# Attention A's relative shift: one write and one read per tile in place of two alternating column halves

## Chip, cores and metric

The kernel runs on one core of one Trainium2 chip. The metric is the time of one execution in device microseconds, lower being better; the median of several runs is quoted.

## What is computed

A block of four layers on x of shape (4, 2048, 256): x plus attention A, plus a feed-forward layer, plus attention B, plus the same feed-forward layer, each on a layer norm of x. Attention A has 16 heads of dimension 16 and relative positions, and it is the layer that the change touches:

```python
def _relative_shift(x):
    b, h, s, _ = x.shape
    x = jnp.pad(x, ((0, 0), (0, 0), (0, 0), (1, 0)))
    x = x.reshape(b, h, s + 1, s)
    return x[:, :, 1:, :].reshape(b, h, s, s)
...
content_score = jnp.einsum('bhsp,bhtp->bhst', q + u, k)
pos_score = jnp.einsum('bhsp,htp->bhst', q + v, pos)
pos_score = _relative_shift(pos_score)
score = (content_score + pos_score) / jnp.sqrt(jnp.float32(P))
weights = jax.nn.softmax(score, axis=-1)
out = jnp.einsum('bhst,bhtp->bhsp', weights, val)
```

The shift puts a zero in front of every row of the 2048 x 2048 matrix of position scores and then reads the same numbers again in rows of 2048. It moves elements between rows by an amount that differs from row to row.

## The kernel before

The four batches run one after the other, and each goes through attention A, feed-forward, attention B and feed-forward. In attention A a batch has 16 heads, a head has 16 tiles of 128 query rows by 2048 keys in f32 (1 MB), so there are 256 tiles to a batch and 1024 in all.

The shift is done by a trip through device memory. The position scores of a tile are computed by TensorE (L522), copied from PSUM to the buffer `rel` in chunks of 512 columns, three by ScalarE (L639) and one by VectorE (L693), and written by DMA to `rel_rows` with a row pitch of S + 1 = 2049 elements. They are read back to the buffer `z` with a row pitch of 2048, starting one row on, which is the shift. `rel` and `z` hold four tiles each (`RING = 4`). VectorE then adds the content scores from PSUM to `z` in two halves of 1024 columns and takes the row maxima (L658, `score`), GpSimd subtracts the maximum (L716), TensorE transposes `z` (L541, `turn`), ScalarE takes the exponential into `pT` (L631) and TensorE multiplies by the values (L562).

Every engine runs the same list of steps s (`in_order`): a prologue of nine steps, a loop of 64 steps (four heads) taken three times, and 64 last steps. In step s each part works on another tile: the position scores on tile s + 9 (`R_LEAD`), the read of `rel_rows` on s + 6 (`Z_LEAD`), the content scores and `score` on s + 4 (`C_LEAD`), the transposes and exponentials on s + 2, the values on s + 1. So a tile is read back three steps after it is written, and scored two steps after it is read.

SyncE (SP) issues every DMA. Its `step` does, in this order: wait until the `z` slot is free (tile n - 4 is transposed, `t_full[3]`), and until tiles n and n + 1 are written (`rel_out`); read half 0 of tile n (L760); wait for the copy of chunk 1 and write half 0 of tile r (L769); read half 1 of tile n; wait for the copies of chunks 2 and 3 and write half 1 of tile r; then, in 12 of 16 steps, two loads of 64 KB for a coming head, and one of 256 KB in one more. A half is 128 rows of 1024 f32, so a transfer has 128 packets of 4 KB, and every one of the 16 DMA engines gets 8 of them. A finished transfer adds 16 to its semaphore, so a tile adds 32 to `rel_out[k]` and 32 to `rel_in[k]` (`moved`). `score` waits for both reads; the copies into a `rel` slot wait for both writes of the tile that had it four tiles ago.

Of the kernel before, what the change touches and what calls it, by code (L numbers as in the profile page):

```python
# [26 lines left out]
P = 128  # L27
# [4 lines left out]
S = 2048  # L32
NT = S // P
# [9 lines left out]
FLAT = S * (S + 1)  # L43
RING = 4
# [10 lines left out]
R_ACT = [0, 1, 2]  # L55
R_DVE = 3
R_FIRST = 3
HB = 4
NB = 2
G = HB * NT  # L60
# [6 lines left out]
OB = 4  # L67
# [12 lines left out]
def program(nc, a, out, nb=4, nh=H):  # L80

    ctx = ExitStack()
    with ctx:
        def sb(name, shape, dt=F32):
            return ctx.enter_context(nc.sbuf_tensor(name, shape, dt))
# [4 lines left out]
        def sem(name):  # L90
            return ctx.enter_context(nc.semaphore(name))
# [8 lines left out]
        rel_d = nc.dram_tensor("rel_rows", (NB, FLAT), F32).ap()  # L100
# [8 lines left out]
        rel = sb("rel", [P, RING, S])  # L109
        z = sb("z", [P, RING, S])  # L110
# [105 lines left out]
        rel_out = [sem(f"rel_out{k}") for k in range(RING)]  # L216
        rel_in = [sem(f"rel_in{k}") for k in range(RING)]
# [6 lines left out]
        QK_INC = 16 * 2 * len(QPART)  # L224
# [6 lines left out]
        def settle(e):  # L231

            e.sem_inc(waited, 1)
# [257 lines left out]
        def in_order(e, b, step):  # L491

            def counts(p):
                return Counts(*(e.snap(b * (nh // HB * per) + p * per)
                                for per in (G, G // OB, 32 * G // RING, HB // NB * QK_INC, HB // NB * 16)))

            with e.Fori(0, 1) as p:
                base = counts(p)
                for s in range(-R_LEAD, 0):
                    step(p, base, s, lambda n: n >= 0)  # L500
            with e.Fori(0, GROUPS - 1) as p:
                base = counts(p)
                for s in range(G):
                    step(p, base, s, lambda n: True)
            with e.Fori(GROUPS - 1, GROUPS) as p:
                base = counts(p)
                for s in range(G):
                    step(p, base, s, lambda n: n < G)

        def moved(base, n):  # L510

            return base.moves + 32 * (n // RING + 1)

        def pe_attn_a(e, b):

# [104 lines left out]
        def act_attn_a(e, b):  # L620

            def step(p, base, s, here):

                r, t = s + R_LEAD, s + T_LEAD
                if here(t):
                    if s >= 0:

                        e.wait_ge(AA["pv_done"], base.tiles + (t - 1))
                    for q in range(4):
                        e.wait_ge(t_full[q], base.tiles + (t + 1))  # L630
                        e.activation(pT[:, t % 2, q * CH:(q + 1) * CH], rg[:, T_BANK[q], :], ACT.Exp,  # L631
                                     scale=SCALE).then_inc(p_ready[q], 1)
                if here(r):
                    if s >= 0 or r >= RING:

                        e.wait_ge(rel_out[r % RING], moved(base, r - RING))
                    for c in R_ACT:
                        e.wait_ge(r_full[c], base.tiles + (r + 1))
                        e.activation(rel[:, r % RING, c * CH:(c + 1) * CH], rg[:, R_BANK[c], :],  # L639
                                     ACT.Copy).then_inc(r_copied[c], 1)  # L640

            in_order(e, b, step)

        def dve_attn_a(e, b):

            def score(p, base, n, half, first):

                ready, read = (("lo_ready", "lo_read"), ("hi_ready", "hi_read"))[half]
                mx = (mlo, mhi)[half][:, n % 2:n % 2 + 1]
                if half == 0:  # L650
                    e.wait_ge(rel_in[n % RING], moved(base, n))
                    if not first:

                        e.wait_ge(AA["nmax_ready"], base.tiles + (n - 1))
                e.wait_ge(AA[ready], base.tiles + (n + 1))
                settle(e)
                zs = z[:, n % RING, 2 * half * CH:2 * (half + 1) * CH]
                e.tensor_tensor_reduce(out=zs, in0=scf[:, 2 * half * CH:2 * (half + 1) * CH], in1=zs, scale=1.0,  # L658
                                       scalar=-3.0e38, op0=ALU.add, op1=ALU.max, accum_out=mx).then_inc(AA[read], 1)
# [65 lines left out]
        def load_pair(e, q, k, q_src, k_src, h, slots, done):  # L725

            for a in slots:
                load_part(e, q, q_src, h, a, QPART[a], done)
                load_part(e, k, k_src, h, a, KPART[a], done)

        def load_v(e, h, hd, done):
            e.dma_start(v_s[hd].rearrange("p t w -> p (t w)"),
                        v_d[bass.ds(h, 1)].rearrange("a p w -> (a p) w")).then_inc(done, 16)

        def sp_attn_a(e, b):

            every = range(SLOTS)
            load_pair(e, qv_s[0], pos_s[0], qv_d, pos_d, 0, every, qv_loaded[0])
            load_pair(e, qu_s[0], k_s[0], qu_d, k_d, 0, every, AA["qk_loaded0"])
            load_v(e, 0, 0, AA["v_loaded0"])  # L740
            load_pair(e, qv_s[1], pos_s[1], qv_d, pos_d, 1, every, qv_loaded[1])

            def read_ready(p, base, n, fresh, last):

                k = n % RING
                if not fresh:

                    e.wait_ge(t_full[3], e.snap(base.tiles + (n - RING + 1)))
                    settle(e)
                e.wait_ge(rel_out[k], e.snap(moved(base, n)))  # L750
                settle(e)
                if not last:
                    e.wait_ge(rel_out[(n + 1) % RING], e.snap(moved(base, n + 1)))
                    settle(e)

            def read_half(n, half):

                k, hd, i0, c0 = n % RING, n // NT % NB, n % NT * P, half * S // 2
                shifted = bass.AP(tensor=rel_d.tensor, offset=hd * FLAT + (i0 + 1) * S + c0, ap=[[S, P], [1, S // 2]])
                e.dma_start(z[:, k, c0:c0 + S // 2], shifted).then_inc(rel_in[k], 16)  # L760

            def write_half(base, n, half):

                k, hd, i0, c0 = n % RING, n // NT % NB, n % NT * P, half * S // 2
                for c in ((R_DVE, R_ACT[-1]) if half else (R_ACT[1],)):
                    e.wait_ge(r_copied[c], e.snap(base.tiles + (n + 1)))
                    settle(e)
                there = bass.AP(tensor=rel_d.tensor, offset=hd * FLAT + i0 * (S + 1) + 1 + c0, ap=[[S + 1, P], [1, S // 2]])
                e.dma_start(there, rel[:, k, c0:c0 + S // 2]).then_inc(rel_out[k], 16)  # L769

            def next_heads(p, base, s, final):

                hd, at = s // NT, s % NT
                nxt = (hd + 1) % NB
                if at in range(1, 7) and not (final and hd + 1 >= HB):
                    if at == 1:
                        e.wait_ge(AA["hi_ready"], e.snap(base.tiles + hd * NT + C_LEAD))
                        settle(e)
                    load_pair(e, qu_s[nxt], k_s[nxt], qu_d, k_d, e.snap(p * HB + (hd + 1)), (at - 1,),
                              AA[f"qk_loaded{nxt}"])  # L780
                if at == 7 and not (final and hd + 1 >= HB):
                    e.wait_ge(AA["pv_done"], e.snap(base.tiles + (hd * NT + V_LEAD)))
                    settle(e)
                    load_v(e, e.snap(p * HB + (hd + 1)), nxt, AA[f"v_loaded{nxt}"])
                if at in range(8, 14) and not (final and hd + 2 >= HB):
                    if at == 8:
                        e.wait_ge(r_full[2], e.snap(base.tiles + (hd + 1) * NT))
                        settle(e)
                    load_pair(e, qv_s[hd % NB], pos_s[hd % NB], qv_d, pos_d, e.snap(p * HB + (hd + 2)), (at - 8,),
                              qv_loaded[hd % NB])  # L790

            def step(p, base, s, here):

                n, r = s + Z_LEAD, s + R_LEAD
                final = not here(G)
                if here(n):
                    read_ready(p, base, n, s < 0 and n < RING, n % NT == NT - 1)
                for half in range(2):
                    if here(n):
                        read_half(n, half)  # L800
                    if here(r):
                        write_half(base, r, half)
                if s >= 0:
                    next_heads(p, base, s, final)

            in_order(e, b, step)


# [640 lines left out]
```

## Time and profile before

| | us |
|---|---|
| median of 3 runs | 11098.51 |
| lowest and highest of them | 11085.86, 11107.45 |
| the profiled execution's own time | 11115.23 |
| its span, first to last instruction | 11113.4 |
| of it: PE, DVE, ACT, POOL busy | 9422.7, 6258.0, 6687.5, 2944.3 |
| TensorE's mean granted clock | 0.947 |

The span is cut by the profile's second part into 40 slices of 278 us, with the busy tenths of each engine, TensorE's granted clock, the mean busy share of the 16 DMA engines and the GB/s that they moved. The groups by line, the waits, the timeline and the table of windows can each be asked of any stretch of the span. In a table of windows the column DMA share is the time of all packets over 16 engines' time; consecutive packets overlap a little, so that it can pass 1.

### The profile page before, as it was taken

Reading aid. Unit: us, or ns where it says so; the run is one execution under the profiler, and the core shown is the slowest. Engines: PE = TensorE matmul, PEld = TensorE weight load, DVE = VectorE, ACT = ScalarE, POOL = GpSimd, SP = SyncE. Lnnn points to the kernel's source line nnn. Section 1 sums busy time; section 2 is a strip of 40 time slices with the busy share of each in tenths; the row PEclk is TensorE's granted clock in tenths of the full one; section 3 lists DMA queues with packets and bytes.
Section 4 is the critical chain, followed back from the end, with each engine's and each line's share of the span. In section 5 each row is a group of like instructions: output and inputs, shape, how many; then the busy total and the mean of one; then the engine's idle time right before and its main releaser. Section 6 shows DMA issues by size and latency. Waiting matters only on the chain. (4 is left out here: it accounts for less than half of the span.)

```text
span 11113.4 us, 271423 instructions
## 1 busy us (share of the span) xinstructions
PE 9422.7 (85%) x95520; PEld 6711.5 (60%) x95520; DVE 6258.0 (56%) x14730; ACT 6687.5 (60%) x11009; POOL 2944.3 (26%) x3520
## 2 busy tenths in 40 slices
PE   5888888999688888899968888889996888888999
PEld 3665665666465666566646656656663565665666
DVE  3655663765365566376446556637644565663764
ACT  3666663765466666376546666637644666663764
POOL 2333332001233333200123333310012333331001
PEclk7999999999899999999989999999998999999999
DMA  6999992000699999100069999911007999991100
GB/s 240 378 363 366 381 378 87 26 25 16 233 377 366 361 379 380 59 25 25 16 254 380 367 362 382 365 46 27 23 18 265 373 372 362 379 357 48 27 22 26
DMA packets 747623, 2482.45 MB, mean 223 GB/s; under 512 B 111745, under 2 KB 133761, under 8 KB 745921
## 3 DMA queue, kind: packets, MB, share of 16 engines
q1 hardware_dynamic: 746176, 2463.84, 60.3%
q8 instruction: 826, 13.53, 0.5%
q14 instruction: 621, 5.08, 0.1%
HBM read 1280.34 MB, written 1183.07 MB: 222 GB/s over the span
## 5 line engine op out<-in xcount | busy, mean ns | idle before, releaser
L658 DVE CUSTOM_DVE_ANT_0 z<-sc,z 128x1024 f32<-128x1024 f32 x2048 | 2496.5, 1220 | 1848.5 <-DMA z<-rel_rows 1608.0
L716 POOL TENSOR_SCALAR z<-z,nmax 128x1024 f32<-128x1024 f32 x2048 | 2277.8, 1123 | 4028.5 <-DVE nmax L668 4028.5
L631 ACT ACTIVATE pT<-rg 128x512 f32<-128x512 f32 x4096 | 2445.9, 598 | 738.7 <-PE rg L541 679.5
L541 PE MATMUL rg<-ident,z 128*128 128x128 f32 x16384 | 2527.0, 277 | 77.0 <-issue 68.3
L639 ACT ACTIVATE rel<-rg 128x512 f32<-128x512 f32 x3072 | 1721.1, 596 | 1407.2 <-PE rg L522 1401.8
L541 PEld LDWEIGHTS rg<-ident,z 128*128 128x128 f32 x16384 | 1990.3, 142 | 784.6 <-ACT rel L639 294.4
L522 PE MATMUL rg<-pos_s,qv_s 96*128 96x512 bf16 x4096 | 1590.8, 396 | 1021.4 <-DVE rel L693 901.6
L1013 DVE CUSTOM_DVE_ANT_0 z<-sc,mask 128x1024 f32<-128x1024 f32 (+7 forms) x1536 | 1359.1, 910 | 227.0 <-PE sc L832 173.9
L952 ACT ACTIVATE pT<-rg 128x512 f32<-128x512 f32 (+3 forms) x1792 | 928.4, 550 | 763.0 <-PE rg L885 751.0
L522 PEld LDWEIGHTS rg<-pos_s,qv_s 96*128 96x128 bf16 x4096 | 478.7, 118 | 1498.0 <-DVE rel L693 1150.9
L960 ACT ACTIVATE z<-z,nmax 128x128 f32<-128x128 f32 (+15 forms) x1024 | 1226.6, 1198 | 89.0 <-POOL nmax L978 76.7
L885 PE MATMUL rg<-ident,z 128*128 128x128 f32 x8704 | 1256.8, 289 | 0.0
L562 PE MATMUL op<-pT,xnT 128*32 128x128 f32 x32768 | 1129.9, 279 | 0.0
L885 PEld LDWEIGHTS rg<-ident,z 128*128 128x128 f32 x8704 | 972.0, 145 | 254.9 <-issue 188.4
L562 PEld LDWEIGHTS op<-pT,xnT 128*32 128x32 f32 x32768 | 847.2, 111 | 243.9 <-issue 214.0
L866 PE MATMUL op<-pT,xnT 128*32 128x128 f32 x17408 | 791.9, 283 | 149.6 <-ACT pT L952 45.5
L693 DVE COPY rel<-rg 128x512 f32<-128x512 f32 x1024 | 702.4, 686 | 183.1 <-PE rg L522 142.4
L866 PEld LDWEIGHTS op<-pT,xnT 128*32 128x32 f32 x17408 | 503.2, 110 | 299.1 <-DVE attn L988 120.6
L534 PE MATMUL sc<-k_sb,xnT 96*128 96x512 bf16 x2048 | 631.2, 390 | 0.0
L534 PE MATMUL sc<-xnT 96*128 96x512 bf16 x2048 | 615.1, 381 | 0.7 <-DVE mlo L658 0.7
L1032 DVE COPY pT<-rg 128x512 f32<-128x512 f32 (+3 forms) x768 | 428.6, 558 | 297.3 <-PE rg L885 288.2
L700 DVE COPY po_sb<-op 128x128 f32<-128x128 f32 x1024 | 298.8, 292 | 494.1 <-PE op L562 493.2
(93 smaller groups left out, 8161.5 us busy)
## 6 DMA issues: line engine op xcount, KB each, us to landing
rel_rows<-rel SPq DMA_DIRECT2D x2048, 512.0 KB, 7.2
z<-rel_rows SPq DMA_DIRECT2D x2048, 512.0 KB, 7.1
xnT<-qu_parts SPq DMA_DIRECT2D x792, 64.0 KB, 2.3
xnT<-v_heads SPq DMA_DIRECT2D x132, 256.0 KB, 4.3
v_heads<-rel SPq DMA_DIRECT2D x8, 4096.0 KB, 12.5
k_sb<-k_parts SPq DMA_DIRECT2D x408, 64.0 KB, 2.3
qv_s<-qv_parts SPq DMA_DIRECT2D x384, 64.0 KB, 6.2
pos_s<-pos_parts SPq DMA_DIRECT2D x384, 64.0 KB, 7.2
```

Of the source, the lines that this page charges most:

```text
L522: e.matmul(rg[:, R_BANK[c], :], qv_s[hd][:, i0:i0 + P], pos_s[hd][:, c * CH:(c + 1) * CH], start=True, stop=True).then_inc(r_full[c], 1)
L534: mm = e.matmul(sc[:, c, :], qu_s[hd % NB][:, i0:i0 + P], k_s[hd % NB][:, c * CH:(c + 1) * CH], start=True, stop=True)
L541: mm = e.transpose(rg[:, T_BANK[q], (j - 4 * q) * P:(j - 4 * q + 1) * P], z[:, n % RING, j * P:(j + 1) * P], ident[:, :])
L562: mm = e.matmul(po[32 * g:32 * g + 32, :], v_s[hd % NB][:, j, :], pT[:, n % 2, j * P:(j + 1) * P], start=j < 4, stop=j + 4 >= NT)
L631: e.activation(pT[:, t % 2, q * CH:(q + 1) * CH], rg[:, T_BANK[q], :], ACT.Exp, scale=SCALE).then_inc(p_ready[q], 1)
L639: e.activation(rel[:, r % RING, c * CH:(c + 1) * CH], rg[:, R_BANK[c], :], ACT.Copy).then_inc(r_copied[c], 1)
L658: e.tensor_tensor_reduce(out=zs, in0=scf[:, 2 * half * CH:2 * (half + 1) * CH], in1=zs, scale=1.0, scalar=-3.0e38, op0=ALU.add, op1=ALU.ma ...
L716: e.tensor_scalar(zs, zs, 1.0, nmax[:, n % 2:n % 2 + 1], ALU.mult, ALU.add).then_inc(AA[done], 1)
L866: mm = e.matmul(po[32 * g:32 * g + 32, :], v_s[t // NT % NB][:, j, :], pT[:, t % 2, j * P:(j + 1) * P], start=j < 4, stop=j + 4 >= nj)
L885: mm = e.transpose(rg[:, B_BANK[q], (j - 4 * q) * P:(j - 4 * q + 1) * P], z[:, t % RING, j * P:(j + 1) * P], ident[:, :])
L960: e.activation(z[:, s % RING, 0:w], z[:, s % RING, 0:w], ACT.Exp, bias=nmax[:, s % 2:s % 2 + 1], scale=SCALE).then_inc(BB["exp_done"], 1)
L1013: e.tensor_tensor_reduce(out=z[:, s % RING, c0:c1], in0=scf[:, p0:p0 + c1 - c0], in1=mask[:, S - width + c0:S - width + c1], scale=1.0, sc ...
```

## The change

The two reads of a tile become one of 256 packets of 4 KB, two to a row, and the two writes become one of 256 such packets. The pattern inside a transfer runs row by row: half 0 of a row, half 1 of the row, half 0 of the next. The bytes, the addresses and the size of a packet stay. Issued per step: one read, then one write. The write waits for chunks 2 and 3 before its first byte goes; the read no longer waits for the copy of chunk 1. A tile now adds 16, not 32, to each semaphore.

```diff
-                                for per in (G, G // OB, 32 * G // RING, HB // NB * QK_INC, HB // NB * 16)))
+                                for per in (G, G // OB, 16 * G // RING, HB // NB * QK_INC, HB // NB * 16)))
...
-            return base.moves + 32 * (n // RING + 1)
+            return base.moves + 16 * (n // RING + 1)
...
-            def read_ready(p, base, n, fresh, last):
-
-                k = n % RING
+            def read_shifted(p, base, n, fresh, last):
+
+                k, hd, i0 = n % RING, n // NT % NB, n % NT * P
...
-            def read_half(n, half):
-
-                k, hd, i0, c0 = n % RING, n // NT % NB, n % NT * P, half * S // 2
-                shifted = bass.AP(tensor=rel_d.tensor, offset=hd * FLAT + (i0 + 1) * S + c0, ap=[[S, P], [1, S // 2]])
-                e.dma_start(z[:, k, c0:c0 + S // 2], shifted).then_inc(rel_in[k], 16)
-
-            def write_half(base, n, half):
-
-                k, hd, i0, c0 = n % RING, n // NT % NB, n % NT * P, half * S // 2
-                for c in ((R_DVE, R_ACT[-1]) if half else (R_ACT[1],)):
+                shifted = bass.AP(tensor=rel_d.tensor, offset=hd * FLAT + (i0 + 1) * S, ap=[[S, P], [S // 2, 2], [1, S // 2]])
+                e.dma_start(z[:, k, :].rearrange("p (a c) -> p a c", a=2), shifted).then_inc(rel_in[k], 16)
+
+            def write_rows(p, base, n):
+
+                k, hd, i0 = n % RING, n // NT % NB, n % NT * P
+                for c in (R_DVE, R_ACT[-1]):
                     e.wait_ge(r_copied[c], e.snap(base.tiles + (n + 1)))
                     settle(e)
-                there = bass.AP(tensor=rel_d.tensor, offset=hd * FLAT + i0 * (S + 1) + 1 + c0, ap=[[S + 1, P], [1, S // 2]])
-                e.dma_start(there, rel[:, k, c0:c0 + S // 2]).then_inc(rel_out[k], 16)
+                there = bass.AP(tensor=rel_d.tensor, offset=hd * FLAT + i0 * (S + 1) + 1, ap=[[S + 1, P], [S // 2, 2], [1, S // 2]])
+                e.dma_start(there, rel[:, k, :].rearrange("p (a c) -> p a c", a=2)).then_inc(rel_out[k], 16)
...
-                    read_ready(p, base, n, s < 0 and n < RING, n % NT == NT - 1)
-                for half in range(2):
-                    if here(n):
-                        read_half(n, half)
-                    if here(r):
-                        write_half(base, r, half)
+                    read_shifted(p, base, n, s < 0 and n < RING, n % NT == NT - 1)
+                if here(r):
+                    write_rows(p, base, r)
```

## Rows read from the trace of the kernel before

**Rows 1.** The page's 40 slices: granted clock, DMA share, GB/s.

```profile
PEclk7999999999899999999989999999998999999999
DMA  6999992000699999100069999911007999991100
GB/s 240 378 363 366 381 378 87 26 25 16 233 377 366 361 379 380 59 25 25 16 254 380 367 362 382 365 46 27 23 18 265 373 372 362 379 357 48 27 22 26
```

**Rows 2.** Windows over attention A of the four batches: busy us by engine, clock, DMA.

```profile
170.00:1680.00 1510.00, 1266.63 (x14399) 899.81 (x14400) 892.53 (x1876) 997.00 (x1757) 556.06 (x500) 0.97 1.00 372
2925.00:4430.00 1505.00, 1265.59 (x14325) 899.79 (x14326) 886.89 (x1865) 990.18 (x1745) 553.09 (x498) 0.97 1.00 371
5690.00:7190.00 1500.00, 1259.28 (x14341) 896.14 (x14342) 888.93 (x1868) 992.06 (x1748) 553.87 (x498) 0.97 1.00 373
8455.00:9960.00 1505.00, 1261.55 (x14325) 895.77 (x14324) 888.12 (x1866) 991.35 (x1749) 552.23 (x497) 0.97 1.00 371
```

**Rows 3.** Windows inside the first batch's attention A, between the loop's jumps.

```profile
1000.00:1400.00 400.00, 342.40 (x3970) 244.94 (x3963) 242.43 (x512) 272.01 (x480) 153.43 (x138) 1.00 1.02 381
...
1100.00:1200.00 100.00, 85.88 (x997) 61.44 (x997) 61.01 (x130) 68.65 (x121) 39.15 (x36) 1.00 1.02 382
```

**Rows 4.** Groups by line from 1100 to 1300 us: busy, mean ns, idle before.

```profile
L658 DVE CUSTOM_DVE_ANT_0 z<-sc,z 128x1024 f32<-128x1024 f32 x68 | 82.9, 1220 | 57.5 <-DMA z<-rel_rows 57.5
```

**Rows 5.** The DMA queue's own waits (SP), 1100 to 1300 us: us, times, longest.

```profile
SPq L233 <- ACT rel L639: 45.1, 64, 1.9
SPq L233 <- PE rg L541: 11.6, 11, 1.8
SPq L233 <- DMA rel_rows<-rel: 4.2, 9, 0.9
```

**Rows 6.** The page's DMA issues: count, KB each, us from issue to landing.

```profile
rel_rows<-rel SPq DMA_DIRECT2D x2048, 512.0 KB, 7.2
z<-rel_rows SPq DMA_DIRECT2D x2048, 512.0 KB, 7.1
```

**Rows 7.** Timeline, 1002.8 to 1013.9 us: start, us, what, [idle before].

```profile
1002.84 1.23 DVE L658 CUSTOM_DVE_ANT_0 z<-sc,z 128x1024 f32<-128x1024 f32 x1 [2.31 <-DMA z<-rel_rows]
...
1004.21 0.34 SPq L760 DMA_DIRECT2D z<-rel_rows  x1
...
1006.34 0.33 SPq L769 DMA_DIRECT2D rel_rows<-rel  x1
...
1006.72 0.61 SPq L760 DMA_DIRECT2D z<-rel_rows  x1
...
1007.54 0.62 SPq L769 DMA_DIRECT2D rel_rows<-rel  x1
...
1008.10 1.22 DVE L658 CUSTOM_DVE_ANT_0 z<-sc,z 128x1024 f32<-128x1024 f32 x1 [1.25 <-DMA z<-rel_rows]
...
1010.45 0.56 SPq L760 DMA_DIRECT2D z<-rel_rows  x1
...
1013.82 1.23 DVE L658 CUSTOM_DVE_ANT_0 z<-sc,z 128x1024 f32<-128x1024 f32 x1 [1.25 <-DMA z<-rel_rows]
```

**Rows 8.** Windows at the start of the first batch's attention A.

```profile
182.00:187.00 5.00, 1.07 (x3) 0.43 (x4) 0.69 (x1) 0.43 (x1) 0.00 (x0) 0.50 1.02 406
...
189.00:192.00 3.00, 0.52 (x2) 0.00 (x0) 0.00 (x0) 0.00 (x0) 0.00 (x0) 0.50 0.99 158
192.00:196.00 4.00, 0.00 (x0) 0.00 (x0) 0.00 (x0) 0.00 (x0) 0.00 (x0) 0.50 1.01 399
```

**Rows 9.** SP's timeline there: six writes, then the first read.

```profile
180.63 5.42 SPq L769 DMA_DIRECT2D rel_rows<-rel  x6
187.62 0.32 SPq L760 DMA_DIRECT2D z<-rel_rows  x1
```

**Rows 10.** One line's instructions over the whole span: ns min/median/max of an issue.

```profile
L769 SPq DMA_DIRECT2D rel_rows<-rel x2048: 314/326/2979, 180.6 to 9971.9; - x187
```

**Rows 11.** The page's DMA packets by size.

```profile
DMA packets 747623, 2482.45 MB, mean 223 GB/s; under 512 B 111745, under 2 KB 133761, under 8 KB 745921
```

**Rows 12.** Windows around a jump back of the loop.

```profile
594.00:598.00 4.00, 0.07 (x1) 0.00 (x0) 0.42 (x3) 0.60 (x1) 1.81 (x2) 0.78 1.04 366
598.00:602.00 4.00, 0.00 (x0) 0.18 (x1) 0.00 (x0) 0.00 (x0) 0.00 (x0) 0.50 0.59 229
602.00:606.00 4.00, 3.40 (x14) 2.59 (x14) 1.34 (x3) 1.20 (x2) 0.00 (x0) 0.50 0.01 4
606.00:610.00 4.00, 4.00 (x52) 2.94 (x50) 2.24 (x5) 2.75 (x6) 1.01 (x1) 0.94 0.26 73
```

## The prediction

> **What bounds the kernel now.** I read the page's slices first [rows 1]. They show four repeats, one per batch, each with some five and a half slices in which the DMA share is 9 tenths or more and 360 to 380 GB/s flow, and then five in which the DMA engines have next to nothing to do. The full stretch is attention A, and only that stretch contains the changed lines. The windows over it [rows 2] give 6020 of the span's 11113 us, at a DMA share of 1.00 from end to end, while TensorE is busy 84% of the time and no other engine over 66%. Away from the ends the share is 1.01 to 1.02 [rows 3], so the 16 engines go from packet to packet without a pause.
>
> A full engine is not yet a bound; the waits must agree. They do [rows 4]: in 200 us VectorE does 68 half scores, that is 34 tiles or 5.88 us a tile, and before them it stands still for 57.5 us, 1.69 us a tile, all put down to the read of `rel_rows`. The bytes say the same. A tile moves 2.097 MB of writes and reads, and a head's 24 loads of 64 KB and one of 256 KB add 1.835 MB over 16 tiles, 0.115 MB each: 2.21 MB, which at the 381 GB/s of [rows 3] takes 5.81 us. So attention A runs at the speed of the DMA engines, and a step's period follows the bytes and their rate. The next bound is near: TensorE is busy 85.88 us in 100 [rows 3], 5.0 us a tile, so no DMA gain can bring more than some 0.8 us a tile, 1024 tiles, 0.8 ms.
>
> The queue has depth as well. From issue to landing a half takes 7.1 to 7.2 us [rows 6], of which its own 0.524 MB at 381 GB/s is 1.4 us; some 5.7 us of other transfers, about 2.2 MB, lie ahead of it. At its waits SP mostly waits for ScalarE's copies (45.1 of 200 us), and for a landed write only 4.2 us [rows 5].
>
> **The change, part by part.** *Bytes, packets, addresses*: the same, 512 packets of 4 KB a tile. At one rate they cost what they cost now.
>
> *Issue on SP*: four issues a tile become two. One takes a median of 326 ns [rows 10], and even if one with twice the packets took twice as long nothing would be lost; SP waits for others anyhow, so I count nothing. Were SP the bound it would be worth up to 2 x 0.33 us a tile.
>
> *The read*: half 1 of the read went out at 1006.72, after SP had waited for a copy and issued half 0 of the write, while half 0 went at 1004.21 [rows 7]. Now all of it goes at 1004.21. VectorE starts that tile at 1013.82, two steps on, and needs both halves. A read 2.5 us earlier in the queue doesn't land 2.5 us earlier for good: with the engines full, landings come one tile per period whatever the order. Counted at nothing.
>
> *The write*: half 0 went out at 1006.34, half 1 at 1007.54 [rows 7]. Now all goes at about 1007.5, 1.2 us later for the first half and no later for the last byte. What is queued behind the longer wait on SP is the head loads and the next step's read, which come after the wait of half 1 today too. What waits for the write's landing is the read two steps on (it needs tile n + 1) and the copy four steps on. In the queue the whole 1 MB of a write now follows a read, not half of it, so it lands some 1.4 us later after that read; z's slot comes free 1.4 us after the score starts (1002.84 to 1004.21 [rows 7]), so the next read may be issued about 1 us later than now. Two whole transfers, 2 MB or 5.5 us, are then still in the queue, so the engines don't run dry. Counted at nothing; without that depth it would be 1 us a tile.
>
> *Completions and changes of direction*: this is what is left. Each DMA engine now goes read, write, read, write within a tile, 8 packets of each, with a completion after each; after the change 16 and 16 with half the completions (the page counts 111,745 packets under 512 B [rows 11], and 16 for each of 4096 of these transfers are 65,536 of them). What does a switch cost? The prologue gives both bounds. SP issues six writes and only then the first read [rows 9]. While only writes flow the rate is 406 GB/s; when the first reads come behind them, there are 3 us at 158 GB/s with the engines counted busy at 0.99; then 399 [rows 8]. So a switch can stall packets, there by (406 - 158) x 3 = 744 KB or 1.8 us. In the steady mix the loss is much less: 2.21 MB at 406 is 5.45 us, against 5.81 at 381, 0.36 us a tile in all. If that loss belonged wholly to the four switches (0.09 us each), two fewer would give 0.18 us a tile, 184 us in all. If it comes from reads and writes being in flight together at all, it stays, and the saving is nothing but some completions whose time no row has. With 2.2 MB, four or five halves, queued ahead and 16 engines working it off independently, both directions are in flight most of the time in either kernel, so I stand near the lower end: a quarter or so, 0.05 us a tile, 1024 x 0.05 = 50 us.
>
> The Trainium skill (DMA: Bandwidth & Descriptors, "Rules for kernel authors") wants transfers of 1 MiB or more and one 128-partition transfer in place of two to disjoint halves. The same page's fit of about 2.0 us fixed plus bytes over 436 GB/s is an estimate of 12.8 us for a tile in four transfers and 8.8 us in two. The 5.88 us of [rows 4] lies under both, so the fixed part is overlapped here and that 4 us is not to be had.
>
> *Prologue, jumps*: at the start of each batch the first read waits for two whole writes; 1.2 us later each, four times, 5 us. At a jump of the loop back the engines run dry for about 8 us [rows 12]; the edit doesn't touch it.
>
> The sum against the profiled execution's own 11115.23: minus 50, 11065. The median of the runs lies 17 us under that execution, so I forecast 11,050.
>
> **The rivals.** *All of the mixing loss belongs to switches*: minus 184 us, 10,915. For it speaks the 158 GB/s stretch; against it, that stretch followed six writes in a row.
>
> *Nothing measurable*: both directions stay in flight together, the rate stays 381, 11,090 or so. For it: the queue's depth. Against: the switch of [rows 8] is visible.
>
> *Slower: a run twice as long makes each switch, or each pair of packets, dearer.* Place: the start of a read run behind a write run, and the write itself, where half 1 of a row now follows half 0 directly and a row ends beside where the next begins. The stall of [rows 8] came after a long run of writes, so stalls may grow with the run. Halving their number only pays while the longer run's switch costs less than twice today's 0.09 us; above 0.18 us it is a loss. For a price I take the slope of [rows 8]: 1.8 us for 3 MB, 0.6 us a MB, so one 1 MB write run 0.6 us of stall a tile in place of today's 0.36 for the whole mix, plus 0.24 us, 246 us: 11,345 at the far end. Half of it, 0.1 us a tile, gives 11,200, the time I give this case.
>
> *The write lands too late and the engines run dry*: the read goes out 1 us late and the 5.5 us of cover fail. 1 ms at worst; 2 in 100, within the chance of slower.
>
> **How the numbers follow.** Chances: my forecast (11,030 to 11,080) 0.35; all of the loss 0.15; nothing measurable 0.27; slower 0.23. A measurement of this kernel tells a difference from about 0.2%, 22 us, so the forecast and the greater gain make faster 0.50, same 0.27, slower 0.23. The range goes down to the greater gain, 10,910, and up to 11,190, short of the price of the slower case; what lies outside is about 2 in 10. The forecast's own range is 11,030 to 11,080.
>
> **What would show it.** In the profile after: GB/s between the jumps rises from 381 to about 384 at a DMA share still of 1.01 to 1.02; VectorE's wait for the read falls from 1.69 to about 1.64 us a tile; the landing time is some 8 us or more for a transfer twice the size; SP waits for landed writes more than 4.2 us in 200; ordinary stretches outside attention A stay the same. I am wrong if GB/s falls at a full share (slower packets), or if the share falls below 1 (the queue runs dry), or if the rate nears 400.

## The result: 2.2% slower, and the profile after

The changed kernel takes 11353.08 us (median of 4 runs, 11314.59 to 11383.07) against 11102.98 us of the kernel before in the same runs: a ratio of 1.0217, 95% interval 1.0197 to 1.0237, 250 us slower. I had forecast 11,050 and faster. The profiled execution's span is 11339.3 us, 226 us longer than before.

The page of the changed kernel: the DMA rows of its 40 slices, the packets by size, and the queue with its packets, MB and share of 16 engines.

```profile
DMA  6999992000599999200069999910007999991000
GB/s 237 366 355 362 363 363 100 26 25 17 205 359 359 353 376 371 90 26 24 16 235 373 353 352 365 366 68 24 24 18 256 368 352 349 362 362 61 24 24 27
DMA packets 452691, 2482.16 MB, mean 219 GB/s; under 512 B 78977, under 2 KB 100993, under 8 KB 188865
q1 hardware_dynamic: 451264, 2463.71, 60.5%
```

Two things are to be seen beside [rows 1] and [rows 11]. In attention A's slices the DMA engines are as full as before, but they move 349 to 376 GB/s where they moved 357 to 382. And there are 452,691 packets where there were 747,623. A tile in two transfers of 256 packets would have lost nothing but half the completions, 32,768 of them. But 452,691 - 188,865 = 263,826 packets are now of 8 KB or more, and 1024 tiles with two transfers of 128 rows are 262,144. (Before there were 747,623 - 745,921 = 1,702 of that size.) So the two halves of a row, which follow one another on both sides of the copy, went as one packet of 8 KB: the change does not do what its words say.

A stretch of attention A between the loop's jumps, in both kernels (the table of windows: busy us of PE, PEld, DVE, ACT, POOL, clock, DMA share, GB/s); before:

```profile
1100.00:1300.00 200.00, 170.54 (x1983) 121.94 (x1983) 121.43 (x257) 136.30 (x240) 77.00 (x70) 1.00 1.01 378
```

after:

```profile
1100.00:1300.00 200.00, 169.40 (x1905) 121.35 (x1898) 116.60 (x246) 130.76 (x230) 73.20 (x66) 0.97 1.01 362
```

The share is 1.01 in both, the rate falls from 378 to 362 GB/s. At 2.21 MB a tile that is 5.85 and 6.10 us, 0.26 us more, and 1024 tiles make it 265 us: about the whole loss. The rate after swings from one 50 us to the next (348 to 388 GB/s between the jumps, with the share at 1.00 to 1.02), so a longer stretch was read as well. From 1060 to 1560 us, before and after:

```profile
1060.00:1560.00 500.00, 429.16 (x4963) 306.97 (x4964) 305.33 (x641) 340.80 (x602) 190.13 (x172) 0.99 1.02 380
1060.00:1560.00 500.00, 423.80 (x4745) 303.67 (x4746) 290.70 (x614) 325.06 (x572) 181.26 (x164) 0.96 1.01 364
```

It says the same: 380 against 364 GB/s, with the share almost unchanged. The engines hardly run dry; the bytes themselves go more slowly.

VectorE's group, its wait and the DMA queue's own waits from 1100 to 1300 us, after, which answer to [rows 4] and [rows 5]:

```profile
L658 DVE CUSTOM_DVE_ANT_0 z<-sc,z 128x1024 f32<-128x1024 f32 x66 | 80.4, 1219 | 60.6 <-DMA z<-rel_rows 51.7 <-PE sc L534 8.8
```

```profile
SPq L233 <- DMA rel_rows<-rel: 50.8, 29, 3.2
SPq L233 <- ACT rel L639: 44.8, 32, 3.5
SPq L233 <- PE rg L541: 21.6, 21, 2.4
```

```profile
rel_rows<-rel SPq DMA_DIRECT2D x1024, 1024.0 KB, 10.2
z<-rel_rows SPq DMA_DIRECT2D x1024, 1024.0 KB, 8.7
```

SP now waits 50.8 us in 200 for landed writes, where it waited 4.2, as forecast, and the read lands 8.7 us after its issue. Neither costs time by itself while the share is full.

### The profile page after: what moved, and what is told of

It is laid out like the page before. It is cut to its first block and busy times, and to the rows that moved or that the text cites. A ratio compares the mean times of both kernels' runs of the same rounds, so it can differ in the third digit from the quotient of the medians.

```text
span 11339.3 us, 268351 instructions
## 1 busy us (share of the span) xinstructions
PE 9517.3 (84%) x95520; PEld 6782.7 (60%) x95520; DVE 6256.7 (55%) x14730; ACT 6685.4 (59%) x11009; POOL 2935.7 (26%) x3520
## 2 busy tenths in 40 slices
DMA packets 452691, 2482.16 MB, mean 219 GB/s; under 512 B 78977, under 2 KB 100993, under 8 KB 188865
## 5 line engine op out<-in xcount | busy, mean ns | idle before, releaser
L541 PEld LDWEIGHTS rg<-ident,z 128*128 128x128 f32 x16384 | 2020.0, 143 | 798.8 <-ACT rel L639 281.4
L562 PE MATMUL op<-pT,xnT 128*32 128x128 f32 x32768 | 1163.0, 285 | 0.0
L878 PEld LDWEIGHTS rg<-ident,z 128*128 128x128 f32 x8704 | 975.7, 145 | 255.6 <-issue 188.3
L562 PEld LDWEIGHTS op<-pT,xnT 128*32 128x32 f32 x32768 | 870.1, 113 | 251.3 <-issue 202.3
L859 PE MATMUL op<-pT,xnT 128*32 128x128 f32 x17408 | 793.9, 284 | 149.0 <-ACT pT L945 45.1
L859 PEld LDWEIGHTS op<-pT,xnT 128*32 128x32 f32 x17408 | 504.0, 111 | 298.5 <-DVE attn L981 120.4
```

The source lines that it names most:

```text
L541: mm = e.transpose(rg[:, T_BANK[q], (j - 4 * q) * P:(j - 4 * q + 1) * P], z[:, n % RING, j * P:(j + 1) * P], ident[:, :])
L562: mm = e.matmul(po[32 * g:32 * g + 32, :], v_s[hd % NB][:, j, :], pT[:, n % 2, j * P:(j + 1) * P], start=j < 4, stop=j + 4 >= NT)
L859: mm = e.matmul(po[32 * g:32 * g + 32, :], v_s[t // NT % NB][:, j, :], pT[:, t % 2, j * P:(j + 1) * P], start=j < 4, stop=j + 4 >= nj)
L878: mm = e.transpose(rg[:, B_BANK[q], (j - 4 * q) * P:(j - 4 * q + 1) * P], z[:, t % RING, j * P:(j + 1) * P], ident[:, :])
```

## The experiments

All medians are compared with runs of the kernel before on the same chip, whose medians lay between 11,101 and 11,122 us. The difference to those is given in brackets. Each diff shows the lines that matter. The semaphore counts that go with them are left out, and so is the matching edit of the read where a run makes it too.

**Order alone, packets of 4 KB.**

```diff
-                for half in range(2):
-                    if here(n):
-                        read_half(n, half)
-                    if here(r):
-                        write_half(base, r, half)
+                if here(n):
+                    read_half(n, 0)
+                    read_half(n, 1)
+                if here(r):
+                    for c in (R_DVE, R_ACT[-1]):
+                        e.wait_ge(r_copied[c], e.snap(base.tiles + (r + 1)))
+                        settle(e)
+                    write_half(base, r, 0)
+                    write_half(base, r, 1)
```

> The changed kernel's order and waits (read, then wait for all copies, then write) with four transfers of column halves and 4 KB packets, as before. If the packets of 8 KB are the cause (the changed kernel's trace has half as many packets as the kernel before), this is back at 11,100, within 0.3%. If the order and the later write are the cause, it stays at 11,350, with SyncE waiting some 50 us in 200 for landed writes. In between, each has its share.

Measured: 11071.58 us (-33), ratio 0.9962, interval 0.9948 to 0.9977. The changed kernel's order and waits, with four column halves, are a small gain and not the loss. Its window:

```profile
1100.00:1300.00 200.00, 173.04 (x1971) 123.97 (x1970) 121.02 (x255) 135.02 (x238) 74.90 (x69) 0.97 1.03 379
```

**The change as it was described.** Gaps in both buffers keep a row as two elements.

```diff
+PAD = 16
...
+        rel_a = rel_t[:, :].rearrange("p (r a c) -> p r a c", r=RING, a=2)
+        z_a = z_t[:, :].rearrange("p (r a c) -> p r a c", r=RING, a=2)
...
+                e.dma_start(z_a[:, k, :, 0:S // 2], shifted).then_inc(rel_in[k], 16)
...
+                e.dma_start(there, rel_a[:, k, :, 0:S // 2]).then_inc(rel_out[k], 16)
```

> The change as it was described: one write and one read a tile, and a gap of 16 elements behind each half row in the buffers, so that a row stays two elements of 4 KB. Packets of 8 KB as the cause: 11,050 to 11,120, and some 590,000 packets of 4 KB and completions instead of 295,000. Order, run length or late write as the cause: 11,350. My predicted gain from fewer switches would show as 11,050.

Measured: 11892.62 us (+788), ratio 1.0714, interval 1.0696 to 1.0732. Its packets and its window:

```profile
DMA packets 714834, 2482.16 MB, mean 209 GB/s; under 512 B 78976, under 2 KB 100992, under 8 KB 713152
```

```profile
1100.00:1300.00 200.00, 162.81 (x1742) 116.75 (x1740) 105.83 (x225) 120.11 (x211) 66.53 (x60) 0.92 1.03 332
```

This is 256 packets of 4 KB, and the rate is 332 GB/s at a share of 1.03. So packets of 8 KB are not needed for a loss; the same bytes in packets of the same size as in the run before this one, walked row by row in one transfer, cost 820 us more. My first theory, the size of the packets, fell here.

**Blocks of 64 rows.** The changed kernel with each transfer, read and write, cut in two, rows 0 to 63 and 64 to 127.

```diff
+                for g in range(2):
+                    g0 = g * (P // 2)
+                    there = bass.AP(tensor=rel_d.tensor, offset=hd * FLAT + (i0 + g0) * (S + 1) + 1, ap=[[S + 1, P // 2], [1, S]])
+                    e.dma_start(there, rel[g0:g0 + P // 2, k, :]).then_inc(rel_out[k], 16)
```

> The changed kernel's order with four transfers of 64 whole rows each, packets of 8 KB. Packets of 8 KB as the cause: 11,350, as the changed kernel. The size of a transfer (256 packets' worth in one piece) as the cause: 11,100. Order as the cause: 11,350 as well, so this is read against the run with column halves in the same order.

Measured: 12543.51 us (+1439), ratio 1.1303, interval 1.1281 to 1.1324. None of my theories gave this number; see the even and odd rows below.

**The write's first half later.** The kernel before, with half 0 of the write behind the copies of all four chunks.

```diff
-                for c in ((R_DVE, R_ACT[-1]) if half else (R_ACT[1],)):
+                for c in (() if half else (R_DVE, R_ACT[-1])):
```

> The kernel before (four column halves, alternating) with one thing moved: half 0 of the write waits for all three copies, as the whole write does after the change, so half 1 of the read is issued later too. If the later write is a cause, it is slower by 50 to 250 us; if packets of 8 KB are the cause, it is 11,100 within 0.3%.

Measured: 11498.85 us (+394), ratio 1.0348, interval 1.0319 to 1.0378. It has both a lower rate and a lower share:

```profile
1100.00:1300.00 200.00, 165.75 (x1852) 118.45 (x1851) 113.74 (x240) 126.86 (x223) 70.53 (x64) 0.96 0.99 353
```

The share is 0.99 where the kernel before has 1.01 in this stretch, the rate 353 GB/s where it has 378; so by this stretch some 2 of the 7% are engines left empty and the rest are slower packets. A later write hurts in this order, where half 1 of the read stands behind the wait. In the order read, read, write, write the same later write did no harm.

**Even and odd rows.** Four transfers of 64 rows again, every second row each, in the read and in the write.

```diff
+                for g in range(2):
+                    there = bass.AP(tensor=rel_d.tensor, offset=hd * FLAT + (i0 + g) * (S + 1) + 1, ap=[[2 * (S + 1), P // 2], [1, S]])
+                    e.dma_start(there, rel[g::2, k, :]).then_inc(rel_out[k], 16)
```

> Four transfers a tile in the changed kernel's order, one with the even rows and one with the odd ones, packets of 8 KB. Blocks of 64 neighbouring rows gave 12,544; if that was because 64 neighbouring partitions meet only a part of the paths into the buffer, spreading the 64 rows over all 128 partitions brings it back to near the changed kernel, 11,350, or to 11,100 if the changed kernel's loss is the size of its transfers. If it stays above 12,000, halving by rows is bad for another reason, the order of the addresses.

Measured: 11034.53 us (-88), ratio 0.9917, interval 0.989 to 0.9944. In the prologue, where only writes flow, blocks of 64 rows:

```profile
183.00:188.00 5.00, 0.00 (x0) 0.00 (x0) 0.23 (x1) 0.00 (x0) 0.00 (x0) 0.50 0.95 261
```

and even and odd rows:

```profile
183.00:188.00 5.00, 2.56 (x7) 0.91 (x8) 0.69 (x1) 1.57 (x3) 0.00 (x0) 0.50 1.02 419
```

A transfer on 64 neighbouring partitions runs at 261 GB/s, one on every second partition at 419. The Trainium skill (SBUF — State Buffer, "Door 1: The DMA port swizzle") says that a DMA's rate depends on how many of the buffer's 16 ports its partitions reach, and its table gives partitions 0 to 63 eight of them. The two rates go that way, though 261 is 0.62 of 419 and not half.

In the changed kernel's write, rows i and i + 1 follow one another; here they never do within a transfer, with the same 8 KB packets, and the kernel is no longer slower than the one before.

**Write or read.** The changed kernel with only its write, then only its read, turned back into column halves.

```diff
+                for half in range(2):
+                    c0 = half * S // 2
+                    there = bass.AP(tensor=rel_d.tensor, offset=hd * FLAT + i0 * (S + 1) + 1 + c0, ap=[[S + 1, P], [1, S // 2]])
+                    e.dma_start(there, rel[:, k, c0:c0 + S // 2]).then_inc(rel_out[k], 16)
```

> The changed kernel with its read (one transfer, 8 KB packets), but the write in two column halves of 4 KB packets, issued one behind the other. If the loss of the change (250 us against the kernel before, 280 against four column halves in the same order) lies in the write, this is near 11,070; if in the read, near 11,350; if it needs both, in between.

> The mirror: the read in two column halves of 4 KB packets, the write in one transfer of 8 KB packets. Loss in the write: near 11,350. Loss in the read: near 11,070.

Measured: with the write in halves 11083.99 us (-38), ratio 0.9962, interval 0.995 to 0.9973. With the read in halves and the write whole 11786.63 us (+664), ratio 1.0602, interval 1.0577 to 1.0627. The loss needs the whole write. Why the whole write costs 414 us more beside a read in halves than beside a whole one is open.

**Only the order of issue.** Read, read, write, write, each write with its own wait as before.

```diff
+                if here(n):
+                    read_half(n, 0)
+                    read_half(n, 1)
+                if here(r):
+                    write_half(base, r, 0)
+                    write_half(base, r, 1)
```

> The kernel before with nothing changed but the order of issue: both halves of the read first, then half 0 of the write behind its own wait, then half 1. The run with this order and one common wait gave 11,072. If that gain comes from the read going out early, it is kept: 11,060 to 11,080. If it comes from the writes following one another directly, it shrinks and this is nearer 11,100.

Measured: 11152.79 us (+30), ratio 1.0024, interval 1.0012 to 1.0037. The transfers stand in the queue in the same order as in the first run, and yet its gain of 33 us is not there. So neither this order nor the earlier second half of the read gives that gain; it needs the common wait before the two writes. In the first run SP waits 34.4 us in 200 for landed writes, here 45.7 us, and a write lands 8.4 and 9.1 us after its issue. By what means the common wait helps is not shown.

**Does the meeting of two rows cost?** With a pitch of 2049 elements a row ends one element before the next begins. If the address space is divided into units of 64 bytes, 112 of the 127 row borders of a tile have the end of one row and the start of the next in one unit (a count from the pitch of 8196 bytes). These three are the changed kernel with another pitch; the read takes the rows of its own tile, so the relative shift is left out.

```diff
-FLAT = S * (S + 1)
+PW = S + 16
+FLAT = S * PW
...
+                shifted = bass.AP(tensor=rel_d.tensor, offset=hd * FLAT + i0 * PW, ap=[[PW, P], [S // 2, 2], [1, S // 2]])
...
+                there = bass.AP(tensor=rel_d.tensor, offset=hd * FLAT + i0 * PW + 1, ap=[[PW, P], [S // 2, 2], [1, S // 2]])
```

> The changed kernel with a row pitch of S + 16 in place of S + 1, for the write and the read (the shift is left out: a tile reads back its own rows, the zero first). A written row still starts 4 bytes past a multiple of 64, but no longer ends in the 64 bytes in which the next begins. If the loss of the change comes from rows written one behind the other that meet within 64 bytes, it goes: 11,020 to 11,080. If it comes from neighbouring rows in one run of writes as such, it stays near 11,350.

> The same with a pitch of S + 128, so that neighbouring rows are 512 bytes apart and share no block of up to 512 bytes (the shift is left out here too). If the unit that must not be shared is larger than 64 bytes, the run with S + 16 stays slow and this one is at 11,020 to 11,080. If both are slow, sharing is not the cause.

> The changed kernel with a row pitch of S for the write, starting at a multiple of 8192 bytes, and the read of the same rows (the shift is left out). Rows follow one another without a gap, but no unit is written in part. If partly written units at the rows' borders are the cause, 11,020 to 11,080; if it is the closeness of the addresses in time, 11,350 or more.

Measured: pitch S + 16, 10848.96 us (-252), ratio 0.9769, interval 0.9749 to 0.9788. Pitch S + 128, 10823.98 us (-277), ratio 0.974, interval 0.9719 to 0.976. Pitch S from an aligned start, 10822.65 us (-278), ratio 0.9735, interval 0.9713 to 0.9757. The page's queue row and the window of the first:

```profile
q1 hardware_dynamic: 451264, 2463.71, 59.2%
```

```profile
1100.00:1300.00 200.00, 178.26 (x2074) 127.71 (x2074) 126.05 (x267) 140.93 (x249) 79.01 (x72) 0.99 1.01 395
```

The same number of packets of the same size, and 395 GB/s in place of 362 at the same share. A gap of 64 bytes between one row's end and the next row's start takes away 502 us; one of 512 bytes brings hardly more. Rows that touch but are aligned are as fast, so it is not the closeness of the addresses. Nor is it that rows begin and end inside a unit, which they do in the first two as well. It is that two rows write into the same 64 bytes, each a part. A larger unit doesn't fit: at S + 16 every second border still lies inside one block of 128 bytes, and that run is only 25 us slower than the one at S + 128. It may be smaller than 64 bytes; no run tells. The read's pitch was changed along with the write's in the first two, but in the third it is the changed kernel's own, and the write in column halves above had already cleared the read.

**A version that beats both.** The read as after the change, the write in even and odd rows, with the real pitch.

```diff
-                e.dma_start(there, rel[:, k, :].rearrange("p (a c) -> p a c", a=2)).then_inc(rel_out[k], 16)
+                for g in range(2):
+                    there = bass.AP(tensor=rel_d.tensor, offset=hd * FLAT + (i0 + g) * (S + 1) + 1, ap=[[2 * (S + 1), P // 2], [1, S]])
+                    e.dma_start(there, rel[g::2, k, :]).then_inc(rel_out[k], 16)
```

> A version to beat both: the read as after the change, one transfer of 128 packets of 8 KB, the write in two transfers of 64 rows, even rows and then odd ones. The run with both directions in even and odd rows gave 11,035, the one with this read and a write in column halves 11,084. If the write alone decides, this is at 11,035; if the read's two transfers helped as well, at 11,080.

Measured: 10968.48 us (-132), ratio 0.9868, interval 0.9845 to 0.9891. It leaves nothing out and is 1.3% faster than the kernel before, better than either value I had expected. Interleaving the rows takes away 382 of the 502 us (from +250 to -132). To the whole write without shared units (-252) 120 us are missing. Even and odd rows still share units across the two transfers, and the column halves below pay 124 us for the same distance; that this is the 120 us is a fit of numbers and not shown.

```profile
1100.00:1300.00 200.00, 177.93 (x2018) 127.67 (x2021) 124.51 (x263) 138.80 (x245) 77.44 (x70) 0.97 1.01 388
```

**The other forms with the wider pitch** (the shift is left out in each).

```diff
-FLAT = S * (S + 1)
+PW = S + 16
+FLAT = S * PW
```

> Four column halves of 4 KB packets in the order read, read, write, write, with the row pitch S + 16 for write and read (the shift is left out). The same order with the real pitch gave 11,072, one whole write and read with pitch S + 16 gave 10,849. If the rows' shared 64 bytes cost nothing where a transfer of halves lies between the two writers, this stays at about 11,070 and the 220 us belong to the whole rows and fewer transfers; if the sharing costs there too, this comes down towards 10,849.

> The kernel before, its order untouched, with the row pitch S + 16 (the shift is left out). Against the changed kernel with this pitch (10,849) it gives what the change does once neighbouring rows share nothing. My forecast's term was a gain of 50 us, with 184 us as its bound: 10,900 to 11,030 here. If the sharing has no cost in alternating halves, it is 11,100.

> The change as described, one write and one read of 256 packets of 4 KB, with the row pitch S + 16 (the shift is left out). The two halves of a row still meet inside one 64-byte unit, 4 bytes past the middle, and are written one behind the other; two rows no longer do. If meeting in a unit is what costs, about half of the 820 us between this form with the real pitch (11,893) and the changed kernel's (11,353)... and 10,849 is left: 11,200 to 11,600. If only rows, not halves, matter, or the 8 KB packets brought nothing, it is near 10,850.

> Four transfers of 64 neighbouring rows with the row pitch S + 16 (the shift is left out). With the real pitch it gave 12,544. If that was shared units, it falls to about 10,850 to 11,100; if it is that 64 neighbouring partitions meet half of the paths into the buffer, it stays above 12,000, or falls only by the 500 us that the changed kernel gained from this pitch.

Measured, with the real pitch beside it, as differences to the kernel before:

| form | pitch S + 1 | pitch S + 16 | ratio and interval at S + 16 |
|---|---|---|---|
| kernel before, alternating column halves | 0 | -29 | 0.9974, 0.9964 to 0.9984 |
| column halves, read, read, write, write | -33 | -157 | 0.9861, 0.984 to 0.9883 |
| changed kernel, 128 packets of 8 KB | +250 | -252 | 0.9769, 0.9749 to 0.9788 |
| one transfer, 256 packets of 4 KB | +788 | +195 | 1.017, 1.0153 to 1.0186 |
| blocks of 64 rows, 8 KB | +1439 | +1296 | 1.1167, 1.1147 to 1.1188 |

The kernel before at S + 16:

```profile
1100.00:1300.00 200.00, 172.45 (x2002) 123.44 (x2004) 123.64 (x260) 137.09 (x242) 75.41 (x68) 0.99 1.02 382
```

Without shared row borders the change would have gained 223 us (-252 against -29). With them it pays 502 us (from -252 to +250), the kernel before 29. The balance is -223 + 502 - 29 = +250; it must come out, since its terms are differences of the same four times. What the runs add is the size of each term. Of the forms tried at both pitches, sharing is cheap (29 us) only in the kernel before, where a read lies between two writes. In the order read, read, write, write, where only another half of the write lies between the two writers of a unit, it costs 124 us (from -157 to -33). Both forms in column halves still meet in the middles of their rows at S + 16, a transfer or more apart. The form with 256 packets of 4 KB keeps one meeting a row at S + 16, in the middle, and stands 447 us above the changed kernel; its 128 meetings a tile are about as many as the changed kernel's 112 shared row borders at the real pitch, which cost 502. With both kinds it is 1040 us above (from -252 to +788), 91 us more than the sum of the two. Blocks of 64 rows stay slow, so theirs is another cause.

## Why the prediction was wrong, point by point

**What bounds the kernel** was right: attention A runs at the rate of the DMA engines at a full share, and the differences show as GB/s from 1100 to 1300 us at shares of 1.01 to 1.03. The exceptions are the write's first half later (0.99) and the blocks of 64 rows (0.96). The first sign of being wrong that the prediction names, GB/s falling at a full share, is what the profile shows.

**The step that failed** is the first of the sum, "Bytes, packets, addresses: the same, 512 packets of 4 KB a tile. At one rate they cost what they cost now." Its premise was false, since a tile now has 256 packets of 8 KB, but that alone costs nothing: at a pitch of S + 16 the same packets give 10,849 us. Its conclusion was false for another reason. The bytes and addresses are the same, but their order in time is not. Alternating column halves keep two writers of one 64-byte unit a transfer or more apart; rows written whole put them directly behind one another. That costs 502 us where I had put nothing. I named the place, a row that "ends beside where the next begins", but only inside the rival for slower, bundled with longer runs and priced by the slope of [rows 8]; its far end, 11,345, lies 8 us from the result by luck, since it was priced from the stall at a change of direction, and the range ended at 11,190. No row of the trace of before shows such a write; only the code does, by its pitch of 2049 elements.

**Completions and changes of direction.** The gain is there and larger than forecast, but its mechanism is not shown. With no row border shared, the changed form is 223 us faster than the old one, where I had 50 us and 184 as the bound. The steps of it at S + 16: the order read, read, write, write with the common wait 128 us (-29 to -157), whole rows in place of halves another 95 us (-157 to -252). At the real pitch the first step was worth 33 us. That fewer changes of direction are what pays is argued and not shown: the first step also moves the write's first half, and at the real pitch the new order without the common wait was 30 us slower. If all 128 us are its own, the term was worth more than twice the 50 us. The 95 us come with no change of direction less. They may be the meetings in the rows' middles, which the column halves have and whole rows in one packet don't, or the longer packets, or the fewer transfers; no run tells them apart.

**Issue on SP, the read's and the write's time.** That an earlier read is worth nothing held: with early writes it was even 30 us slower. Two issues fewer were not tried by themselves; at S + 16 they are a part of the 95 us. The later write didn't run the engines dry in the new order, as forecast, though SP waited for landings twelve times as long. In the old order it does, +394 us, which I had not asked.

**The rivals.** "Slower" came true by its second mechanism. "The change doesn't do what it says" had no chance in my list, and it belonged there: a count of packets would have settled it.

Left open: why the whole write costs more beside a read in halves (+664) than beside a whole read (+250), and how much of the +394 is the lower rate and how much the lower share. By what means two writes into one unit hold each other up is open too; the runs show that they do, and that it costs little where a read lies between them. The runs at other pitches read back other rows than the real shift does, but write and read as many bytes in transfers of the same shape, and the run at pitch S keeps the read's pitch. In the form with 4 KB packets the size of the packet changes along with the meetings, so its 447 us are theirs only by the agreement of the numbers.

## What to carry to other kernels

When a stage runs at a full DMA share, look not at how many transfers there are but at the order in which addresses are written: writes directly behind one another that each touch a part of the same 64 bytes cost some 0.5 us a tile of 128 rows here, and interleaving the rows (even, then odd) took away 382 of 502 us for one more issue. Where the rows can be padded so that they share no unit, that is better still; here the shift's read runs on from one row into the next and forbids it. Try reads together and writes together with one wait before the writes (33 us here, 128 us with padded rows), and count the packets in the profile after, since neighbouring elements merged. Don't cut a transfer into blocks of 64 neighbouring partitions, which cost 1439 us here; take every second one.

## What the runs showed of the hardware that I had not expected

- An access pattern of two contiguous 4 KB elements a row went as one packet of 8 KB (452,691 packets in place of 747,623).
- Meetings of two partial writes in 64 bytes: 502 us for 112 shared row borders a tile, 447 us (by comparison of forms, packet size included) for 128 meetings in the rows' middles, 124 us where half a write lies between, 29 us where a read lies between as well.
- With writes alone they hardly show: in the changed kernel's prologue the rate is 408 GB/s, at pitch S + 16 it is 407 and at the two other pitches 418 in the same five microseconds. With reads beside them it was 362 against 395.

```profile
182.00:187.00 5.00, 2.09 (x5) 0.74 (x6) 0.69 (x1) 1.45 (x3) 0.00 (x0) 0.50 1.00 408
```

- 64 neighbouring partitions: 261 GB/s, 64 alternate ones: 419.
